# A graph network on one core: indirect DMAs of the sort and the scoring limited to two in flight

## What is computed

```python
msg_src = node_input @ W_src + b_src
msg_dst = node_input @ W_dst
kv = msg_src[edge_src] + msg_dst[edge_dst]
h = silu(edge_scalars @ W_fc1 + b_fc1); h = silu(h @ W_fc2 + b_fc2); w = h @ W_fc3 + b_fc3
tp = kv * edge_attr * w
kv2 = (tp @ W_kv + b_kv).reshape(-1, 2 * N_HEADS, HEAD_DIM)
alpha = einsum('ehd,ehd->eh', q[edge_dst], kv2[:, :N_HEADS])
...                                  # softmax of alpha over the edges of a dst, weighted sum of v
```

## Time and profile before

| | us |
|---|---|
| median of three runs | 16656.17 |
| lowest and highest | 16643.24, 16665.29 |
| span of the profiled execution | 19335.7 |
| sort, scatters from first to last (in it) | 615.5 to 5741.0 |
| scoring, gathers from first to last (in it) | 6133.1 to 9049.4 |
| POOL busy in the span | 8860.6 (46%) |
| PE, DVE, ACT busy in the span | 11298.7, 10446.0, 4413.4 |

### The profile page before, as it was taken

The page is one execution under the profiler, slowest core; times in us unless marked ns, Lnnn a source line. Parts: engine busy times, 40 slices in busy tenths (PEclk is TensorE's granted clock), DMA queues, the critical chain, the costliest instruction groups (busy, mean ns, idle before and its releaser), DMA issues. The chain is left out here.

```text
span 19335.7 us, 330621 instructions
## 1 busy us (share of the span) xinstructions
PE 11298.7 (58%) x72558; PEld 8581.2 (44%) x72559; DVE 10446.0 (54%) x36907; ACT 4413.4 (23%) x11783; POOL 8860.6 (46%) x9490
## 2 busy tenths in 40 slices
PE   5555555555545666564475666656555665446886
PEld 4333333333324555554375444433224553225776
DVE  7655555555542333333464777772345445777776
ACT  0011111111101222221011342006201112445665
POOL 0456556556551555555674344530362444333332
PEclk9766766667665666666555566765555555557887
DMA  7622222222222222223233798757543776665554
GB/s 313 253 63 65 63 64 63 62 65 63 65 59 69 58 57 57 57 57 56 50 58 33 249 312 271 214 169 241 174 127 89 228 224 213 216 216 175 174 173 142
DMA packets 2143987, 2588.95 MB, mean 134 GB/s; under 512 B 892151, under 2 KB 1761472, under 8 KB 2143848
## 3 DMA queue, kind: packets, MB, share of 16 engines
q1 hardware_dynamic: 1755208, 1752.17, 31.5%
q0 software_dynamic: 353792, 654.90, 11.6%
q10 hardware_dynamic: 34848, 180.49, 2.3%
HBM read 1738.16 MB, written 848.30 MB: 134 GB/s over the span
## 5 line engine op out<-in xcount | busy, mean ns | idle before, releaser
L556 POOL DMA_INDIRECT edges_by_dst<-rec,pos x1568 | 1527.2, 974 | 2135.3 <-DVE rec L491 1694.2
L989 POOL DMA_INDIRECT sc_rows<-src_table,sc_idx x1664 | 1581.9, 951 | 1484.8 <-DVE sc_tp L1087 813.7
L556 POOL DMA_INDIRECT edges_by_cell<-rec,pos x1568 | 1532.7, 977 | 528.7 <-issue 528.4
L1734 PE MATMUL ex_rows<-table,ex_oh 128*128 x6528 | 1173.5, 348 | 821.1 <-DVE ex_oh L1702 423.8
L1820 PE MATMUL gs_part<-gs_rows,gs_oh 128*128 128x192 bf16 x6528 | 1100.8, 332 | 787.6 <-DVE gs_oh L1793 309.3
L1039 PE MATMUL sc_loc<-dst_table,sc_ohT 128*128 x3328 | 767.1, 403 | 1140.3 <-ACT sc_ohT L1005 1097.2
L1782 POOL DMA_INDIRECT gs_rows<-rows_by_src,chunk_read_by_src x1088 | 1059.9, 974 | 778.2 <-PE gs_part L1820 474.6
L2221 PE MATMUL at_part<-cell_edge_term,key_in_block 128*66 128x128 f32 x8704 | 1218.1, 304 | 252.4 <-issue 201.2
L1734 PEld LDWEIGHTS ex_rows<-table,ex_oh 128*128 128x128 bf16 x6528 | 752.1, 132 | 1242.2 <-issue 1202.7
L520 DVE SCALAR_TENSOR_TENSOR junk<-rowb,keycol,earlier 128x128 f32<-128x128 f32 (+1 forms) x3136 | 1151.4, 413 | 240.5 <-issue 236.3
L2221 PEld LDWEIGHTS at_part<-cell_edge_term,key_in_block 128*66 128x66 f32 x8704 | 1132.0, 158 | 323.5 <-issue 302.9
(11 more groups left out here) (393 smaller groups left out, 25910.8 us busy)
## 6 DMA issues: line engine op xcount, KB each, us to landing
ex_keys<-src_key_rows SPq DMA_DIRECT2D x1632, 128.0 KB
rows_by_src<-ex_stage SPq DMA_DIRECT2D x1088, 192.0 KB
rowb<-sort_key_rows SPq DMA_DIRECT2D x392, 512.0 KB
ex_keys<-dst_key_rows SPq DMA_DIRECT2D x1088, 128.0 KB
dst_rows_by_src<-patY ACTq DMA_DIRECT2D x1, 104448.0 KB
gs_rows<-dst_rows_by_src SPq DMA_DIRECT2D x544, 192.0 KB
scored_dst_rows_by_src<-patZ ACTq DMA_DIRECT2D x1, 71808.0 KB
scored_rows_by_src<-ex_stage SPq DMA_DIRECT2D x544, 132.0 KB
```

The costliest lines, as they stand in the source:

```text
L556: nc.gpsimd.indirect_dma_start(out=out, out_offset=bass.IndirectOffsetOnAxis(ap=pos[:, u, k, j:j + 1], axis=0), in_=row, in_offset=None).t ...
L989: nc.gpsimd.indirect_dma_start(out=rows[:, u, j, :], out_offset=None, in_=tabS, in_offset=bass.IndirectOffsetOnAxis(ap=idx[:, u, j:j + 1], ...
L1734: m = nc.tensor.matmul(rows[k][u % 2][r // 2][:, r % 2, 0:W], oh[k][:, u % 2, r * P:(r + 1) * P], t3[:, bass.ds(held[k][u], 1), :].rearran ...
```

## The change

Each indirect DMA of the two stages waits for an earlier one. In the sort the semaphores are no longer one for each half `u` but one for each list (`scattered_by_dst`, `scattered_by_cell`), and each scatter waits until all scatters before it to its own list have landed: the last but one in the order of issue. In the scoring the four semaphores of the ring become two, for even and odd `j`, and each gather waits for all before it of its own parity. Each has a wait and a nop of its own, in place of one nop a group. All who waited for a group's DMAs (SP at L452, ACT at L998, DVE at L1085, POOL at the end) now wait on both semaphores. The first turn of the sort's loop on POOL is unrolled, so that no wait for zero is made in the loop.

```diff
-        s_sc = [sem(f"scattered{u}") for u in range(2)]
+        s_sc = [sem(f"scattered_by_{x}") for x in ("dst", "cell")]
...
-                            sp.wait_ge(s_sc[u], (after + 1) * 2 * SG * 16)
+                            for k in range(2):
+                                sp.wait_ge(s_sc[k], (after * 2 + u + 1) * (SG * 16))
                             sp.sem_inc(s_free, 1)
...
-                with pool.Fori(0, NG // 2) as i:
+                def scatter(i):
                     for u in range(2):
                         g = i * 2 + u
                         pool.wait_ge(s_pos, g + 1)
                         pool.wait_ge(s_rec, g + 4)
-                        pool.nop(nofuse=True)
                         for j in range(SG):
                             for k, out, row in ((0, A, rec[:, u, j, :]), (1, Al, rec[:, u, j, DST:DST + 4])):
+                                wait(pool, s_sc[k], (g * SG + j) * 16)
+                                pool.nop(nofuse=True)
                                 nc.gpsimd.indirect_dma_start(
                                     out=out, out_offset=bass.IndirectOffsetOnAxis(ap=pos[:, u, k, j:j + 1], axis=0),
-                                    in_=row, in_offset=None).then_inc(s_sc[u], 16)
+                                    in_=row, in_offset=None).then_inc(s_sc[k], 16)
+                scatter(0)
+                with pool.Fori(1, NG // 2) as i:
+                    scatter(i)
...
-        s_ga = [sem(f"sc_gathered{u}") for u in range(RING)]
+        s_ga = [sem(f"sc_gathered{b}") for b in range(2)]
...
-                    pool.nop(nofuse=True)
                     for j in range(G):
+                        wait(pool, s_ga[j % 2], g * (G // 2 * 16) + j // 2 * 16)
+                        pool.nop(nofuse=True)
                         nc.gpsimd.indirect_dma_start(out=rows[:, u, j, :], out_offset=None, in_=tabS,
-                                                     in_offset=bass.IndirectOffsetOnAxis(ap=idx[:, u, j:j + 1], axis=0)).then_inc(s_ga[u], 16)
+                                                     in_offset=bass.IndirectOffsetOnAxis(ap=idx[:, u, j:j + 1], axis=0)).then_inc(s_ga[j % 2], 16)
...
-                    wait(act, s_ga[u], i * 16 * G)
+                    for b in range(2):
+                        wait(act, s_ga[b], (g - RING + 1) * (G // 2 * 16))
...
-                    dve.wait_ge(s_ga[u], (i + 1) * 16 * G)
+                    for b in range(2):
+                        dve.wait_ge(s_ga[b], (g + 1) * (G // 2 * 16))
```

More of the change, by code:

```diff
@@ L552, in _ @@
                         pool.wait_ge(s_rec, g + 4)
-                        pool.nop(nofuse=True)
                         for j in range(SG):
                             for k, out, row in ((0, A, rec[:, u, j, :]), (1, Al, rec[:, u, j, DST:DST + 4])):
+                                wait(pool, s_sc[k], (g * SG + j) * 16)
+                                pool.nop(nofuse=True)
                                 nc.gpsimd.indirect_dma_start(
                                     out=out, out_offset=bass.IndirectOffsetOnAxis(ap=pos[:, u, k, j:j + 1], axis=0),
-                                    in_=row, in_offset=None).then_inc(s_sc[u], 16)
-                for u in range(2):
-                    pool.wait_ge(s_sc[u], NG // 2 * 2 * SG * 16)
+                                    in_=row, in_offset=None).then_inc(s_sc[k], 16)
+                scatter(0)
+                with pool.Fori(1, NG // 2) as i:
+                    scatter(i)
+                for k in range(2):
+                    pool.wait_ge(s_sc[k], NG * SG * 16)
             @block.scalar
```

## The result

| | before | changed |
|---|---|---|
| median, us | 16660.73 | 18829.83 |
| lowest and highest | 16643.24, 16672.31 | 18827.44, 18838.95 |
| runs | 4 | 4 |

The ratio is 1.131, with a 95% interval from 1.1296 to 1.1323: the change costs 2169 us.

The account below looks back on a forecast made before the run. POOL was taken to pace both stages in timed runs. Scatter pairs 580, SP's loads 235, fills 70 and gathers 545 sum to 1430; added to 16,656 that gives 18,085 us, range 16,620 to 18,850.

Parts of the forecast that it names:

- What bounds the stages: Sort and scoring: in timed runs POOL sets the pace, at 20.2 and 5.0 us a group.
- the silences: Idle stretches of engines other than POOL in sort and scoring, taken to come with profiling; 5.23 and 7.81 us in two rows.
- rival C: Both stages: timed runs have the profile's slack too, so the waits fit in it; 16,656 to 16,750 us, chance 0.15.
- Rival D: Both stages: the handed-over queue holds up other engines' signals and two in flight end that; faster, 16,070 us, chance 0.10.
- The instruction itself: A wait and a nop before each of 3136 scatters and 1664 gathers on POOL: costs nothing.
- The pair of scatters: Sort: landing 2.15 plus restart 0.75 makes 2.90 us against 2.53, +580 us; bounds +235 and +740.
- The fills: Sort, 616 to 768 us, DMA engines at 0.92: some six groups have slower pairs; +70 us, at most 150.
- Scatters that meet SP's loads: Sort, each group's start: one or two of eight pairs land late, 1.2 us a group, +235 us; bounds 0 and 500.
- The gathers: Scoring: a pair takes 3.20 us against 2.51, +545 us; bounds +110 and +1020.
- Rival B: Both stages: in undisturbed runs the scatters' completion hides within 2.53 us a pair; 17,040 us, chance 0.11.
- The signs: Changed kernel's profile: scatter pairs near 2.9 us, gather pairs near 3.2, sort group 24.4 to 27, nothing changed after 9060 us.

Follow-up runs that it names:

- undisturbed profile: The kernel before, unchanged, profiled a second time on a chip of the first kind: 16,690.72 us, span 16,689.0.

## Why the prediction was right, and where it was off

**What bounds the stages: right, for a wrong reason.** POOL at 20.2 and 5.0 us a group, estimated for the timed runs, is 20.8 and 5.1 in the undisturbed profile. But the silences don't come "with profiling": the two stages take 1841 us more in the earlier trace rows than on the first kind, and two chips are some 2400 us slower in their timed runs too. On those the kernel before has, by the estimate above, the slack of the profile, and rival C was about them: there the waits fit in it in part, and the change costs 514 us rather than 2169. I had laid a difference between two numbers on the profiler that lay between two chips. The forecast for the profile of the changed kernel, a span of 19,300 to 20,000, was wrong with it: that profile has 18,825.7 us. Only on a chip of the second kind is it 19,627.6, and there too the stages need 28.6 and 6.9 us, not 24.4 and 6.4.

**Rival D: a true mechanism, too small a price.** Two in flight does end the silences (above). It would have paid if the waits alone had cost 24.4 and 6.4 us a group. At 28.6 and 6.9, held against the earlier trace rows, the sort loses 488 us and the scoring wins 50. With the burst's waits taken out (25.0 us) the gain is there: 1.2% faster than before, on that kind of chip.

**The instruction itself: nothing.** Right: 0.9999.

**The pair of scatters: right.** 2.90 predicted, 2.96 measured: 0.43 x 1568 = 674 us, where the forecast has 580. Restart and landing are those of the earlier trace rows.

**The fills: right.** POOL does 49 instructions from 616 to 768 us (97 before). At 28.6 / 16 = 1.79 us a scatter 49 would take 88 us, so the fills cost 64; before, 97 x 1.265 = 123 of the 152 leave 29. The difference is 35, within "at most 150" and half of the 70.

**Scatters that meet SP's loads: wrong, by the factor 3.5.** This is the step that failed. 1532 - 674 - 35 = 823 us are left for them, 4.2 us a group, where I took 1.2 (235 us), with a bound of 500. This is what is left over, but the trace has it directly as well: from the 16th group on, the first four steps of a group take 10.4 us in the mean, 4.5 over two undisturbed pairs, of which the kernel before loses 0.4 too. I had reckoned that one or two pairs land late, by 0.6 to 1.2 us each. The row has a POOL that stands for 5.40 us before one scatter. That the loads meet the first scatters of a group isn't new: SP waits for a group's last scatters in both kernels, and its loads start 1.2 to 1.4 us after a group's first scatter in the undisturbed profile of before, 0.7 to 1.0 in the changed kernel. What is new is that POOL waits for these landings with nothing left in its queue, and a megabyte and more at 181 GB/s takes most of 8 us. I had the size of the burst in hand, 5.5 us of the DMA engines a group (0.21 of 26.1; one burst's 8.00 us have 5.0), and yet took 1.2 us, which came from no row.

**The gathers: mechanism right, size short.** The pair is 2840.5 / 832 = 3.41 us, not 3.20, and 710 us rather than 545. The lower of the two rows of the stage itself (2.50 in the earlier trace rows) plus 0.75 gave 3.25; the upper (3.02) 3.77. The mean lies between them, nearer the lower.

**Rival B** is out: from one scatter's start to the start of the next that waited for it are 2.96 us, not 2.53 or less. The Trainium skill (DMA: Bandwidth & Descriptors, Anatomy of one DMA, SWDGE path) gives a fixed cost of about 2.0 us for one such DMA. The trace agrees if that figure leaves the restart out: 2.96 less the restart of 0.75 are 2.2 us.

**The signs.** Pairs near 2.9 and 3.2 came (2.96 and 3.41). A sort group at 24.4 to 27 us did not (28.6), for the reason above.

The sum: 674 + 823 + 35 + 710 = 2242, less the 105 in the untouched stages, is 2137 by the profiles, 2169 by the timed runs. The total lay 745 us above the forecast and only 20 us within the range. That it is within is luck in part: the loads alone exceed their bound (500) by 323 us, and the fills and the gathers, far below theirs (150 and 1020), leave room for it. It also took chips of the first kind: on the other the changed kernel has 19,629 us.

## What to carry to other kernels

A limit on DMAs in flight is free as long as their number times the issue time exceeds landing plus restart (here 4 x 1.265 us against 3.0), and costs the difference on each DMA as soon as the issuing engine sets the pace. With four in flight the scoring is within 11 us of the kernel before; the sort, where landings are later than that once a group, is 361 us longer. Count the worst landing, not the usual one: look at what else is released by the same event and will stand in the DMA engines before the waited-for transfer, and price it by the time that the whole burst takes. Where a profile's span is far from the timed median, take a second profile before laying the difference on the profiler; it can be another chip, on which the same change has another price.

## What the chip showed that I had not expected

- Two kinds of chips: the same kernel takes 16,643 to 16,693 us on some and 19,063 to 19,143 us on two, steady on each. The changed kernel takes 18,830 and 19,629.
- On the second kind stages with much DMA traffic are longer and carry less per us (the same later stage of the changed kernel, first on the first kind, then on the second; the last two figures are DMA share and GB/s):

```profile
14993.00:16052.00 1059.00, 792.70 (x13005) 710.27 (x13002) 642.59 (x2709) 238.38 (x1084) 528.94 (x544) 0.66 0.88 272
```

```profile
15253.00:16518.00 1265.00, 809.61 (x13003) 728.40 (x12999) 621.70 (x2708) 225.32 (x1084) 526.32 (x544) 0.59 0.79 228
```

- In the first profile, which fits the second kind, engines other than POOL stand still while a long row of indirect DMAs is handed over (1497 us of ACT's time in the scoring, up to 18.0 at once), and with two in flight they don't on that kind. Six scatters in a row that wait for no landing bring one silence of 6.1 us in the whole sort there; ten bring many, shorter than those of the first profile. The four-in-flight kernel was not run there, nor is it shown what in the chip holds the signals up.
